# Queries made in transposed form, two chunks at a time, in a linear-attention and expert kernel on one core

## What is computed

```python
def _phi(x, omega):
    proj = jnp.einsum('bhnd,md->bhnm', x, omega)
    norm = 0.5 * jnp.sum(x * x, axis=-1, keepdims=True)
    return jnp.exp(proj - norm) / math.sqrt(M)
...
q, k, v = _heads(x @ wq.T), _heads(x @ wk.T), _heads(x @ wv.T)
phi_q, phi_k = _phi(q, omega), _phi(k, omega)
kv_cumsum = jnp.cumsum(jnp.einsum('bhnm,bhnd->bhnmd', phi_k, v), axis=2)
k_cumsum = jnp.cumsum(phi_k, axis=2)
out = jnp.einsum('bhnm,bhnmd->bhnd', phi_q, kv_cumsum)
z = 1.0 / (jnp.einsum('bhnm,bhnm->bhn', phi_q, k_cumsum) + 1e-06)
out = (out * z[..., None]).transpose(0, 2, 1, 3).reshape(b, n, H * D)
return out @ wo.T + bo
```

## Time and profile before

| | us |
|---|---|
| runs | 727.14, 727.89 (median), 730.52 |
| profiled execution | 727.18 |
| its span on the core | 725.1 |
| opening, up to step 0 | 0 to 27.6 |
| step 0 | 27.6 to 41.7 |
| steps 1 to 30 | 41.7 to 543.0 |
| step 31 | 543.0 to 554.0 |
| closing steps, hand over to the experts | 554 to 575 |
| experts and the sum at the end | 575 to 725.1 |

### The profile page before, as it was taken

The page is one execution under the profiler, slowest core; times in us unless marked ns, Lnnn a source line. Parts: engine busy times, 40 slices in busy tenths (PEclk is TensorE's granted clock), DMA queues, the critical chain, the costliest instruction groups (busy, mean ns, idle before and its releaser), DMA issues. The chain is left out here.

```text
span 725.1 us, 27349 instructions
## 1 busy us (share of the span) xinstructions
PE 697.4 (96%) x11452; PEld 604.1 (83%) x11452; DVE 536.0 (74%) x1685; ACT 387.6 (53%) x740; POOL 335.6 (46%) x625
## 2 busy tenths in 40 slices
PE   8999999999999999999999999999999789999956
PEld 8788888888888888888888888888887779999942
DVE  6687888878878887888878878888775456565416
ACT  5755566665656665666656566665552144544310
POOL 3002545555544445454545554545447306556550
PEclk9999999999999999999999999999999999999989
DMA  9974000000000000000000000000000154553128
GB/s 252 362 268 178 11 9 11 10 9 11 14 15 10 11 10 11 10 10 11 9 11 11 14 14 9 11 11 11 10 11 14 49 177 130 168 173 113 51 82 304
DMA packets 32705, 47.25 MB, mean 65 GB/s; under 512 B 4132, under 2 KB 20168, under 8 KB 32584
## 3 DMA queue, kind: packets, MB, share of 16 engines
q1 hardware_dynamic: 23296, 32.62, 13.4%
q0 software_dynamic: 4096, 8.42, 3.6%
q10 hardware_dynamic: 5192, 4.47, 1.9%
HBM read 22.21 MB, written 23.36 MB: 63 GB/s over the span
## 5 line engine op out<-in xcount | busy, mean ns | idle before, releaser
L1297 POOL DMA_INDIRECT y_rows<-y_sb,row_id x64 | 62.8, 982 | 66.0 <-DVE y_sb L1442 49.9
L1108 POOL DMA_INDIRECT dispatched<-h_cur,slot x64 | 67.3, 1051 | 17.8 <-issue 16.1
L1376 ACT ACTIVATE hidden<-bank,b_col 128x512 f32<-128x512 f32 x64 | 43.3, 689 | 58.2 <-PE bank L1348 57.8
L632 ACT ACTIVATE phi_k<-expo_k 128x1024 f32<-128x1024 f32 x32 | 33.9, 1058 | 74.5 <-DVE expo_k L768 70.7
L648 ACT COPY v_sb<-bank 128x512 f32<-128x512 f32 x64 | 37.6, 587 | 62.1 <-PE bank L279 58.7
L527 PEld LDWEIGHTS bank<-woT,attT 128*128 128x128 f32 x512 | 61.9, 192 | 3.2 <-ACT attT L738 0.6
L859 DVE TENSOR_TENSOR scores<-bank,within 128x512 f32<-128x512 f32 x64 | 41.2, 686 | 31.2 <-PE bank L310 31.2
L527 PE MATMUL bank<-woT,attT 128*128 128x128 f32 x512 | 62.4, 275 | 0.4 <-ACT attT L738 0.4
L1317 PE MATMUL bank<-w_sb,hidden 128*128 128x128 f32 x512 | 59.7, 275 | 0.8 <-issue 0.8
L137 POOL TENSOR_TENSOR rs<-var,power 128x1 f32<-128x1 f32 x64 | 37.1, 579 | 49.8 <-DVE var L132 49.5
L1317 PEld LDWEIGHTS bank<-w_sb,hidden 128*128 128x128 f32 x512 | 58.3, 192 | 1.2 <-issue 1.2
(11 more groups left out here) (243 smaller groups left out, 2037.9 us busy)
## 6 DMA issues: line engine op xcount, KB each, us to landing
dispatched<-blank SPq DMA_DIRECT2D x16, 524.0 KB, 3.1
region<-dispatched SPq DMA_DIRECT2D x30, 262.0 KB, 2.9
y_rows<-blank SPq DMA_DIRECT2D x8, 512.0 KB, 3.9
w_nat<-in_L_ffn_w_dram SPq DMA_DIRECT2D x8, 256.0 KB, 3.7
y_got<-y_rows SPq DMA_DIRECT2D x8, 256.0 KB, 6.8
y_got<-y_rows ACTq DMA_DIRECT2D x8, 256.0 KB, 7.4
out_dram<-x_sb SPq DMA_DIRECT2D x8, 256.0 KB, 3.7
w_sb<-in_L_ffn_w_dram ACTq DMA_DIRECT2D x6, 256.0 KB, 2.8
```

The costliest lines, as they stand in the source:

```text
L1108: pool.indirect_dma_start(out=dispatched[:, :], in_=h2_cur[par][:], in_offset=None, out_offset=bass.IndirectOffsetOnAxis(ap=slot[par][:, k ...
L1297: pool.indirect_dma_start(out=y_rows[:, :], out_offset=bass.IndirectOffsetOnAxis(ap=row_id[par][:, t:t + 1].bitcast(U32), axis=0), in_=y_s ...
L1376: act.activation(hidden[par][:, k, :], psum[2 + k][:], ACT.Gelu, bias=b1_col[:, bass.ds(e * KH + k, 1)]).then_inc(sem(f"hid{k}_out"), 1)
```

## The change

The queries are no longer projected as tokens x features and then turned. `project_qT` makes them turned at once (weights stationary, the tokens of two chunks moving, 256 columns), half of the heads in one step and half in the next. ScalarE copies them to qT, VectorE squares that, and `exponent_qT` makes omega q - |q|^2 / 2 in PSUM by two products per head, one with omega and one with a table of -1/2. ScalarE's exponential writes phiT_q directly. The pq weights, the pq projection, the transposes of phi_q, and the reduction and exponents of q on VectorE are gone. k's features carry 1/M, since q's carry nothing. h is made four chunks ahead in place of two, and has three buffers of two chunks. The projections stand in two groups, q and k at the head of the step, v and pk in its middle; between them stand attend_state, attend and the first state_gain. pk, k, and the scores now share banks 2 and 3. GpSimd's scatter stands before the second norm.

```diff
-                TURNS = {0: ["q0", "k0", "v0", "pq0", "pk0"], 1: ["q1", "k1", "v1", "pq1", "pk1"],
-                         2: ["tk0", "tk1", "a0", "attT0"], 3: ["tq0", "tq1", "a1", "attT1", "rank"],
+                TURNS = {0: ["q0", "v0", "pq0"], 1: ["q1", "v1", "pq1"],
+                         2: ["tk0", "k0", "pk0", "a0", "attT0"], 3: ["tk1", "k1", "pk1", "a1", "attT1", "rank"],
                          4: ["o0", "o2", "h2T", "lg"], 5: ["o1", "o3"],
-                         6: ["late0", "hT", "late1"], 7: ["early0", "early1", "wo"]}
+                         6: ["hT", "late0", "late1"], 7: ["early0", "early1", "wo"]}
...
+                        def project_qT(n):
...
+                            for side in range(2):
...
+                                for i in range(2):
+                                    o = q_bank(side, n)[:, i * 2 * P:(i + 1) * 2 * P].rearrange("p (c t) -> p c t", t=P)
+                                    cols = slice(side * 512 + (first + i) * P, side * 512 + (first + i + 1) * P)
+                                    pe.matmul(o, wT_hi["q"][:, cols], hi, start=True, stop=False)
+                                    pe.matmul(o, wT_lo["q"][:, cols], hi, start=False, stop=False)
+                                    mm = pe.matmul(o, wT_hi["q"][:, cols], lo, start=False, stop=True)
+                                mm.then_inc(sem(f"q{side}_in"), 1)
+
+                        def exponent_qT(n, c):
...
+                            pe.wait_ge(sem("q_squared"), n + 1)
+                            for i in range(2):
+                                for w, of in ((omT, qT), (minus_half, qT_square)):
+                                    for side in range(2):
+                                        for r in range(2):
+                                            cols = slice(side * 512 + i * 2 * P, side * 512 + (i + 1) * 2 * P)
+                                            mm = pe.matmul(q_bank(r, n)[half_rows(side), i * 2 * P:(i + 1) * 2 * P],
+                                                           w[half_rows(r), :], of[half_rows(r), cols],
+                                                           start=(w is omT), stop=(w is minus_half), skip_group_check=True)
...
                         def score(g, c, par):
 
 
                             if g == 0:
-                                pe.wait_ge(sem("tk1_out"), c + 1)
-                                pe.wait_ge(sem("tq1_out"), c + 1)
+                                for half in range(2):
+                                    pe.wait_ge(sem(f"tk{half}_out"), c + 1)
+                                    pe.wait_ge(sem(f"pq{half}_out"), 2 * (c // 2) + 2)
+                                    if live(c, 1):
+                                        pe.wait_ge(sem(f"pk{half}_out"), c + 2)
...
+                                if live(c, 4):
+                                    pe.wait_ge(sem("hT_out"), c + 5)
                             else:
                                 pe.wait_ge(sem("gain0_out"), c + 1)
-                                if live(c, 2):
-                                    pe.wait_ge(sem("hT_out"), c + 3)
...
+                            features_T(0, c, par)
+                            features_T(1, c, par)
+                            if live(c, 4):
...
+                                pe.transpose(psum[BANK["hT"]][:, 0:P], xn[par][:], ident[:]).then_inc(sem("hT_in"), 1)
+                            if live(c, 2):
+                                project_qT(c + 2)
...
                             if tail:
                                 attend_state(1, c - 1, nxt, (j - 1) % CPB)
+                                attend(1, c - 1, nxt, (j - 1) % CPB)
                             state_gain(0, c, par, j)
-                            if tail:
-                                attend(1, c - 1, nxt, (j - 1) % CPB)
                             if front:
-                                project("v0", c, nxt)
-                                project("v1", c, nxt)
+                                project("v0", c)
+                                project("v1", c)
+                                project("pk0", c)
+                                project("pk1", c)
                             score(0, c, par)
                             score(1, c, par)
+                            if live(c, 2):
+                                exponent_qT(c + 2, c)
...
                             if last:
                                 routing_rank(c)
-                            if front:
-                                project("pk0", c, nxt)
-                                project("pk1", c, nxt)
                             if tail:
                                 add_heads(c)
...
+                            if back:
+                                features_T_out(0)
+                                features_T_out(1)
+                            if live(c, 2):
+                                qT_out(c + 2)
+                            if front:
+                                squares_k(c)
+                            if live(c, 4):
+                                shift_scale(c + 4)
+                            if front:
+                                values(c)
+                                exps_k(c, nxt)
...
+                            if live(c, 2):
+                                exps_q(c + 2)
...
+                        def square_q(n):
+
+                            dve.wait_ge(sem("q1_out"), n + 1)
+                            dve.tensor_tensor(qT_square[:], qT[:], qT[:], ALU.mult).then_inc(sem("q_squared"), 1)
...
+                            exponent_qT(0, -1)
+                            exponent_qT(1, -1)
...
+                                if last:
+                                    scatter()
                                 rstd(pool, "ln2", var2, rs2, c)
```

More of the change, by code:

```diff
@@ L273, in project @@
                             cols = slice(half * 512, (half + 1) * 512)
-                            first = HALF if half and w in ("k", "pk", "v") else 0
+                            first = HALF if half else 0
                             toks = slice(first, first + P)
-                            pe.matmul(o, twice(h_hi[par])[:, toks], wT_hi[w][:, cols], start=True, stop=False)
-                            pe.matmul(o, twice(h_hi[par])[:, toks], wT_lo[w][:, cols], start=False, stop=False)
-                            pe.matmul(o, h_lo[par][:, toks], wT_hi[w][:, cols], start=False, stop=True).then_inc(sem(kind + "_in"), 1)
@@ L281, in features_T @@
[L281 to L293 removed]
+                            pe.matmul(bank[:], hi_of(n)[:, toks], wT_hi[w][:, cols], start=True, stop=False)
@@ new lines, in project, with features_T @@
+                            pe.matmul(bank[:], hi_of(n)[:, toks], wT_lo[w][:, cols], start=False, stop=False)
+                            pe.matmul(bank[:], lo_of(n)[:, toks], wT_hi[w][:, cols], start=False, stop=True).then_inc(sem(kind + "_in"), 1)
+                        def features_T(half, c, par):
+                            if half and c >= 3:
+                                pe.wait_ge(sem("rank_out"), c - 2)
+                            elif c >= 2:
+                                pe.wait_ge(sem(f"attT{half}_out"), c - 1)
+                            elif c == 1:
+                                pe.wait_ge(sem(f"a{half}_out"), 1)
+                            pe.wait_ge(sem("phi_k_ready"), c + 1)
@@ L634, in shift_scale, with qT_out @@
-                        def shift_scale(c, b, j, par):
-                            act.wait_ge(sem("hT_in"), c + 3)
-                            act.wait_ge(sem("h_split"), c + 2)
-                            own = bass.ds(b + (j + 2) // CPB, 1)
-                            rows = psum[7 if c < 0 else BANK["hT"]][:, 0:P].unsqueeze(1).to_broadcast([P, 2, P])
+                        def qT_out(n):
+                            act.wait_ge(sem("pq1_in"), n)
+                            for side in range(2):
+                                act.wait_ge(sem(f"q{side}_in"), n + 1)
+                                act.copy(qT[:, side * 512:(side + 1) * 512], q_bank(side, n)[:]).then_inc(sem(f"q{side}_out"), 1)
@@ new lines, in squares_k, with exps_q @@
+                        def squares_k(c):
+                            act.wait_ge(sem("norm_k_ready"), c + 1)
+                            for half in range(2):
+                                act.wait_ge(sem(f"k{half}_in"), c + 2)
+                                act.activation(square_k[:, half * 512:(half + 1) * 512], k_bank(half, c)[:],
+                                               ACT.Square).then_inc(sem(f"k{half}_out"), 1)
+                        def exps_q(n):
+                            pairs = phiT_q[n // 2 % 2][:, n % 2 * 4:n % 2 * 4 + 4, :].rearrange("p (s r) t -> p r s t", r=2)
+                            for r in range(2):
+                                act.wait_ge(sem(f"pq{r}_in"), n + 1)
```

(12 more changed lines are left out.)

406 lines of the change are left out of this document (198 added, 208 removed).

## The result

| | before | changed |
|---|---|---|
| median, us | 727.51 (726.0 to 730.52, 4 runs) | 803.0 (801.35 to 804.11, 4 runs) |
| profiled execution, us | 727.18, span 725.1 | 801.35, span 799.5 |
| TensorE busy, us | 697.4 | 706.8 |

The ratio is 1.103, with a 95% interval of 1.0988 to 1.1072. The forecast was 782 (762 to 803), slower with a chance of 0.93: the sign and the mechanism in the loop were right, the size was 21 us short. The median is the last value of the range, and two of the four runs lie above it.

The account below looks back on a forecast made before the run. TensorE, busy all through the loop, was taken as the bound, so any wait on it adds time. Work -23.5, stalls +32.2, +20.2, +23.2 and opening chain +2.8 make +54.9 on 727.18: 782 us, range 762 to 803.

Parts of the forecast that it names:

- The work on TensorE, -0.69 a step: Each loop step: pq projection, phi_q transposes and two group starts go, q loads and exponent_qT come; -0.69 us.
- The disputed term: exponent_qT's sixteen matmuls each step: 1.75 us from two-by-two quadrant rows; the skill's 3.07 gain would make 2.1 us.
- The prediction's 0.16 for two starts of a group: TensorE, each step: k follows q and pk follows v directly, saving 2 x 0.09, about 0.16 us.
- The waits: 1.04, 0.65, 0.83: TensorE stalls per step: score after pk 1.04 us, add_heads (wo) for VectorE's state 0.65, state_gain(0) for ScalarE's h 0.83.
- the first rival: Waits do not bind: TensorE runs ready matmuls past a waiting one, all three waits vanish; 706 us, chance 0.05.
- The second rival: Only the wait at score binds; ScalarE's h and VectorE's additions come early; 739 us, chance 0.06.
- the third: Quadrants with 256 columns run two at a time, so exponent_qT costs 3.5 us; 838 us, chance 0.06.
- the fourth: A queue called on time is late (VectorE's chain or the step's tail); 792 to 810 us, chance 0.10.
- The opening, +4.9: Before the loop: +2.1 us of TensorE work, +2.8 as exponent_qT(1) waits for exponent_qT(0), two copies and a square.
- The rest, -0.3: From step 31 on: step 31 loses only transposes, -0.9 us, and has one add_heads stall of 0.65; later stages untouched.
- I cost it at nothing: GpSimd's scatter moved forward delays h2 by two transfers; h2 is wanted late in the step, so priced at nothing.
- The likeliest case: The three stalls and work as priced: 782 us, own range 768 to 796, chance 0.73.

Follow-up runs that it names:

- four edits: Changed kernel with shift_scale first and increment ahead of attend(1), half the exponent ahead of the scores, half of phi_k's transposes ahead of wo, scatter at its old place: 737.95 us.
- own buffers in the opening: The kernel with shift_scale, exponent, transpose and scatter moves, plus separate buffers for chunk 1's qT and its square: 731.95 us.

## Why the prediction was right, and by how much it was short

**The work on TensorE, -0.69 a step: -0.54.** The step of 18.72 less the three stalls as measured (1.03, 0.65, 0.81) is 16.23, against 16.77. (The prediction's terms make a step of 18.54, not its 18.4.) The disputed term was well sized: exponent_qT takes 1.73 us, four times 0.43, where I took 1.75, and leaving half of it out gave back 0.86. (To the start of the next group, with its change of shape, it is 1.87.) One after another its 32 passes of 256 columns would take 6.85 us by the 0.107 per 128 columns of the earlier trace rows, so the quadrants give 3.96 times the rate. The Trainium skill's measured 3.07 for four row tiles ("TensorE: Matmul & The Clock Gate", Measured speedup vs the span model) would make 2.2 us, an estimate (the prediction has 2.1); no run here has four row tiles, and the two-by-two quadrants of this trace took 1.73. The q projection cost +0.04 (316.51 to 318.02), as taken. Missing is 0.15 us at the heads' matmuls, 1.86 instead of 1.71, for which I had no term. The trace puts half of it at each end. Their second pass starts 0.184 us after the first where it was 0.108, since the first weight load now starts behind the wait too, 0.03 ahead of the first matmul where it was 0.23 ahead (PEld, changed kernel, then before):

```profile
313.71 0.19 PEld L599 LDWEIGHTS bank<-woT,attT 128*128 128x128 f32 x1 [0.57 <-issue]
...
306.13 0.42 PEld L527 LDWEIGHTS bank<-woT,attT 128*128 128x128 f32 x2
```

And from their last pass to the next group it is 0.112 us, as between all other passes, where the projection of q followed after 0.031. The prediction's 0.16 for two starts of a group counted the longer first matmul of a projection (0.09) and not the shorter pass ahead of it (0.08).

**The waits: 1.04, 0.65, 0.83.** Measured 1.03, 0.65 and 0.81; removing them one at a time gave 0.87 (all that the cover was long), 0.45 (the same) and 0.80. Every price from before carried over, and the first rival fell: during no wait did a matmul that stood behind start. The Trainium skill (the same page, The mechanism) has matmuls start and end in strict program order, and the trace agrees at all three waits. The second rival fell with them and the third with the exponent's 1.73; the fourth, a queue late that I had called on time, did not happen in the loop as written.

**The whole loop.** The terms for steps 1 to 30 make +49.1; measured +54.4. Of the 5.3 us, 30 times 0.15 of work at wo are 4.5; three of the thirty steps lack the wait at wo, 2 us the other way, so that some 3 us are not traced.

**The opening, +4.9 (2.1 of work, 2.8 of chain): +9.3.** The chain was sized right (2.57 for 2.8) and the work not contradicted. What failed is that I read only the new exponents there and not what TensorE's shorter list would uncover. It reaches the weights of k and v earlier, waits 1.37 us for their DMA, and does the next 16 transposes in 3.2 us, where the same 16 took 1.7 before, at a granted clock of 0.53 (TensorE in order of time, then the window of that stretch):

```profile
12.69 1.82 PE L501 MATMUL bank<-ident,wk_nat 128*128 128x128 f32 x8 [1.37 <-DMA wv_nat<-in_L_attn_wv_dram]
14.30 1.91 PE L501 MATMUL bank<-ident,wv_nat 128*128 128x128 f32 x8
```

```profile
12.70:15.90 3.20, 3.20 (x16) 3.11 (x16) 1.43 (x3) 1.67 (x3) 0.00 (x0) 0.53 1.15 302
```

With 0.75 us of waits for VectorE's xn that makes 3.6 of the 4.4. The kernel before has no low clock in its opening (1.00). This split is of one execution: in the profiles of the seven kernels with the same opening, step 0's transpose of xn stands at 38.69 to 40.84 us, here at 37.81.

**Step 0, +1.2 (-0.69 + 1.04 + 0.83): +3.5.** There TensorE waited 1.69 us for h_hi, idle time alone, where a full step has 0.28, the matmuls behind ran at a lower clock for some 3 us (the windows of the last section), and the stop without a releaser took 1.23. The prediction spoke of the clock in the loop alone, and there it stayed at 1.00; what it costs outside had no term.

**The rest, -0.3 (-0.9 and one wait at wo of 0.65): +7.2.** The step that failed is "I cost it at nothing", on the scatter. A late h2 is hidden by a full step's projections, and step 31 has none: 4.14 us, and a lower clock behind. Putting the scatter back gave 2.9 us by the medians; in the profiles the stretch from step 31 on is about 3.4 us shorter. The other 3.7 us of the rest stand at its very end, behind the experts' last block, which the prediction called untouched: TensorE's wait for the gathered rows (y_got) is 3.0 us where it was 1.4, the 28 transposes behind it take 13.3 us from the first start to the last where they took 11.7, and the clock is low for longer. The run with the scatter put back has this too (2.8 and 13.4 us). No run shows why.

So the sum was short by 5.3 in the loop and by 14.2 at its two ends. There, the 3.7 us without a cause apart, I had priced the change's own work and not the cover that it took away. The likeliest case had ended at 796; the range held because it took in the fourth rival, whose cause, a late queue in the loop, was not there. That 803.0 still lies in it is luck.

**And without the waits?** The four edits leave a step at 16.61, only 0.16 below the kernel before: splitting the exponent costs a second start of a group (0.17), and the transposes ahead of wo take 0.64 us to its first matmul instead of 0.44 (316.90 to 317.54 and 319.40 to 319.84 in the run with four edits). That last 0.20 is a rest of the wait, without idle time in the trace: in the steps where no state is carried on it is missing, and they take 16.35. With own buffers in the opening it is 731.95 against 728.0, 1.0022 to 1.0066 times. No version here beats the kernel before. In the profile of the best one the opening and step 0 take 46.9 us against 41.7, steps 1 to 30 497.2 against 501.3, and the rest 185.9 against 182.1: the loop now gains 4 us, and both ends lose more.

## What to carry to other kernels

On an engine that is busy all the time, moving an instruction next to the one whose result it needs costs the round trip through the other engine, less what still stands between, and rows of the kernel before, from the last matmul to the first behind a wait, priced it here to 0.02 us. Price the cover at both ends of a loop too: a transfer or a chain that costs nothing in a full step shows in the first and the last one. When several waits are filled, look for the chain of the other engines just behind: here it was reached when all three were filled.

## What the runs showed of the hardware that I had not expected

In the changed kernel the granted clock fell after single long stops outside the loop, to 0.50 (1.2 of 2.4 GHz), and never in steps 1 to 30, with three idle pieces of up to 0.97 us in each step. The run with four edits, around its stop of 2.57 us at 32.0 to 34.6:

```profile
33.00:35.00 2.00, 0.39 (x8) 0.39 (x12) 1.76 (x3) 1.19 (x3) 0.00 (x0) 0.96 0.98 400
35.00:37.00 2.00, 2.00 (x25) 1.50 (x21) 1.86 (x5) 0.00 (x0) 0.00 (x0) 0.50 0.92 365
37.00:39.00 2.00, 2.00 (x20) 1.24 (x13) 0.21 (x2) 0.86 (x2) 0.55 (x1) 0.68 0.70 272
```

The changed kernel has the same stop at the same place (32.4 to 35.0) and kept 1.00 there, alone among the eight profiles with this opening, but fell to 0.50 after its 1.69 us in step 0:

```profile
35.00:37.00 2.00, 2.00 (x33) 1.41 (x34) 1.90 (x5) 0.01 (x1) 0.00 (x0) 1.00 0.95 377
...
41.00:43.00 2.00, 0.41 (x26) 0.44 (x30) 1.61 (x2) 1.44 (x3) 0.48 (x1) 1.00 0.81 327
43.00:45.00 2.00, 2.00 (x25) 1.61 (x17) 0.86 (x2) 0.41 (x1) 0.12 (x1) 0.65 0.85 346
45.00:47.00 2.00, 2.00 (x6) 1.54 (x6) 0.00 (x0) 0.76 (x2) 0.00 (x0) 0.50 0.95 293
```

The run with four edits, in turn, kept 1.00 through its stop of 3.10 us in step 0 and behind it:

```profile
50.00:53.10 3.10, 0.02 (x2) 0.00 (x0) 0.59 (x2) 0.00 (x0) 0.00 (x0) 1.00 0.73 283
```

So the length of a stop alone does not decide it, and executions of the same opening can differ by 3 us.
